# Rotary embedding in a fused decoder: exchanging the halves with a DVE shuffle instead of with products

## The reference, cut to what matters

```
def apply_rope(t, freqs):
    rot = freqs.shape[-1]                        # 32
    t1, tp = (t[..., :rot], t[..., rot:])
    d2 = rot // 2
    rh = jnp.concatenate([-t1[..., d2:], t1[..., :d2]], axis=-1)
    t1 = t1 * jnp.cos(freqs) + rh * jnp.sin(freqs)
    return jnp.concatenate([t1, tp], axis=-1)

q = (xq @ Wq).reshape(b, n, HEADS, DH).transpose(0, 2, 1, 3) * DH ** (-0.5)   # DH = 64: 0.125
k = (ctx @ Wk).reshape(b, j, HEADS, DH).transpose(0, 2, 1, 3)
v = (ctx @ Wv).reshape(b, j, HEADS, DH).transpose(0, 2, 1, 3)
q, k = apply_rope(q, pe_q), apply_rope(k, pe_k)
sim = jnp.where(mask, einsum('bhid,bhjd->bhij', q, k), -max)
out = einsum('bhij,bhjd->bhid', softmax(sim), v) -> reshape(b, n, 512) @ Wo + bo
```

## Time and profile before

| | |
|---|---|
| median of 3 runs | 4510.98 us (4506.9 to 4514.82) |
| the profiled execution | 4516.42 us, span of its trace 4514.8 us |
| PE busy | 89% of the span, 23856 matmuls |
| DVE / ACT / POOL busy | 59% / 44% / 19% |
| mean granted TensorE clock | 0.955 |

### The profile page before, as it was taken

How to read it: one execution, slowest core, us unless ns; L and a number is a source line. 1 busy time by engine, 2 the same in 40 slices (tenths; PEclk the granted TensorE clock), 3 DMA queues, 4 the chain that set the end, 5 groups by cost and what they waited for, 6 DMA issues and landing times. The chain is left out here.

```text
span 4514.8 us, 70500 instructions
## 1 busy us (share of the span) xinstructions
PE 4015.5 (89%) x23856; PEld 2483.2 (55%) x23856; DVE 2675.4 (59%) x7163; ACT 1998.7 (44%) x5804; POOL 860.4 (19%) x972
## 2 busy tenths in 40 slices
PE   6887799999999988889968877999999999888898
PEld 4644445655555555555646444565555555555555
DVE  3677566666666644654346775666666666456543
ACT  1732435555445434663227214454554444346632
POOL 2145221122221200000021452211122212000000
PEclk7999999999999998999969999999999999999999
DMA  2000000000000010010010000000000000100000
GB/s 68 24 16 1 16 7 16 22 16 22 16 22 1 25 54 19 7 57 8 1 57 5 16 1 16 7 16 22 16 22 16 22 2 24 54 20 34 30 8 10
DMA packets 15847, 91.84 MB, mean 20 GB/s; under 512 B 2176, under 2 KB 8064, under 8 KB 12032
## 3 DMA queue, kind: packets, MB, share of 16 engines
q1 hardware_dynamic: 15488, 87.27, 5.3%
HBM read 86.22 MB, written 1.05 MB: 19 GB/s over the span
## 5 line engine op out<-in xcount | busy, mean ns | idle before, releaser
L559 PE MATMUL ps_O<-wide,V 128*64 128x256 f32 (+4 forms) x5152 | 596.5, 394 | 1.9 <-ACT wide L583 1.8
L628 ACT ACTIVATE EX<-NB,neg 128x154 f32<-128x154 f32 (+3 forms) x640 | 350.2, 551 | 399.4 <-DVE neg L653 399.2
L601 POOL COPY RX<-recips 128x256 f32<-128x256 f32 (+2 forms) x356 | 156.8, 440 | 1822.9 <-DVE recips L668 1757.2
L679 DVE TENSOR_TENSOR QT<-ps_O,RS 128x512 f32<-128x512 f32 x212 | 146.6, 692 | 444.3 <-PE ps_O L559 444.3
L510 PE MATMUL ps_S<-KT,QT 64*128 64x154 f32 (+7 forms) x1936 | 368.0, 463 | 31.8 <-issue 21.5
L583 ACT ACTIVATE wide<-ps_P 128x512 f32<-128x512 f32 (+2 forms) x648 | 367.6, 569 | 60.9 <-PE ps_P L541 60.8
L394 POOL TENSOR_TENSOR small<-small 128x4 f32<-128x4 f32 x112 | 113.5, 1013 | 1467.8 <-DVE small L379 955.1
L541 PE MATMUL ps_P<-consts,EX 128*128 128x128 f32 (+1 forms) x2148 | 317.3, 281 | 80.0 <-ACT wide L583 41.5
L559 PEld LDWEIGHTS ps_O<-wide,V 128*64 128x64 f32 (+4 forms) x5152 | 266.9, 127 | 194.5 <-issue 110.7
L510 PE MATMUL ps_OUT<-KT,QT 64*128 64x154 f32 (+5 forms) x968 | 336.0, 441 | 0.4 <-ACT EX L628 0.4
L585 DVE COPY wide<-ps_P 128x512 f32<-128x512 f32 (+4 forms) x404 | 259.3, 643 | 117.9 <-PE ps_P L541 117.5
(11 more groups left out here) (345 smaller groups left out, 8154.1 us busy)
## 6 DMA issues: line engine op xcount, KB each, us to landing
weights<-in_w_dram SPq DMA_DIRECT2D x10, 1664.0 KB, 6.8
weights<-in_w_dram SPq DMA_DIRECT2D x2, 6148.0 KB, 17.5
weights<-in_w5next_dram SPq DMA_DIRECT2D x6, 1664.0 KB, 6.8
weights<-in_w_dram SPq DMA_DIRECT2D x2, 4200.0 KB, 13.0
weights<-in_reltab_dram SPq DMA_DIRECT2D x2, 4096.0 KB, 12.3
weights<-in_w_dram SPq DMA_DIRECT2D x8, 640.0 KB, 3.9
weights<-in_w_dram SPq DMA_DIRECT2D x5, 832.0 KB, 4.4
weights<-in_w_dram SPq DMA_DIRECT2D x2, 2050.0 KB, 8.0
```

The lines of the kernel that those rows point to most:

```text
L559: ins = pe.matmul(O1[self.slot * j:self.slot * (j + 1), q0 * P:(q0 + self.nq) * P], self.value(c * self.hpc + j, kc), self.probs(rd, j)[:, ...
L601: pool.tensor_copy(RX[:, q0 * P:(q0 + self.nq) * P].rearrange("p (n s) -> p n s", s=self.slot), of.unsqueeze(2).broadcast_to([P, self.nq * ...
L628: ins = act.activation(ex[:, a * N:(a + 1) * N], src, ACT.Exp, bias=neg[:, at:at + 1], scale=-1.0 if self.added else 1.0, accum_out=sums[: ...
L679: dve.tensor_tensor(self.out_chunk(c), O1[:, :], RS[:, c % 2, :], ALU.mult).then_inc(r.av_sb, 1)
```

## The change

The swapped products go. A chunk is now one row of the table, of the kind "rope": its product is read twice from the PSUM bank by DVE, first by a shuffle that exchanges lanes 0 to 15 with 16 to 31 in every group of 32 partitions and writes the part buffer, then by the multiplication with cos. POOL multiplies the part by sin (for queries by `sinq`, sin times 0.125, made once) and then, after a wait for its own result, adds. Groups of 32 channels that are not rotated are shuffled too; their sin is zero. Shuffle and cos row are evacuated in DVE's order; the shuffle of chunk j waits for POOL's rotation of chunk j - 4. In self steps the order of chunks is now k0, q0, k1, q1, ..., and scores of head pair c wait for 2c + 2 rotations; in cross steps it stays. All chunks still come before the first scores on PE and DVE. `fill2` goes: all value rows stand before the scores of round 1, the last one behind a wait for the next lane's `XT`, in self and cross steps. The weights are packed and loaded as before, the swapped ones too.

```
+        HALVES = [(m + 16) % 32 for m in range(32)]
+        def rope(dve, r, bank, dst, part, tables, wait):
+            if wait:
+                dve.wait_ge(*wait)
+            dve.stream_shuffle(part, bank, HALVES).then_inc(r.evac_dve, 1)
+            if tables[0] is None:
+                dve.tensor_tensor(dst, bank, tables[1], ALU.mult).then_inc(r.evac_dve, 1)
+            else:
+                dve.scalar_tensor_tensor(dst, bank, tables[0], tables[1], ALU.mult, ALU.mult).then_inc(r.evac_dve, 1)
...
-                self.order = [("k", c) for c in range(4)] + [("q", c) for c in range(4)]
+                self.order = [("k", c) for c in range(4)] + [("q", c) for c in range(4)] if cross else \
+                    [(m, c) for c in range(4) for m in "kq"]
...
-                                     queries=lambda c: (self.r.rotated, 4 + c + 1))
+                                     queries=lambda c: (self.r.rotated, 4 + c + 1 if cross else 2 * c + 2))
...
-                return [([(self.w("w" + m)[:, c * P:(c + 1) * P], x)], P, n, "D", kind, self.dest(m, c), cos),
-                        ([(self.w("swap" + m)[:, c * P:(c + 1) * P], x)], P, n, "D", kind, self.part[j % 4][:, 0:n],
-                         sin, (self.r.rotated, j - 3) if j >= 4 else None)]
+                return ([self.product(j)], P, n, "D", "rope", self.dest(m, c), (self.part(j), self.tables(j), self.before(j)))
+
+            def rotate(self, pool, j):
...
+                pool.wait_ge(r.evac_dve, 2 * j + 2)
+                pool.tensor_tensor(part, part, sin, ALU.mult).then_inc(r.sum_step, 1)
+                pool.wait_ge(r.sum_step, j + 1)
+                pool.tensor_tensor(d, d, part, ALU.add).then_inc(r.rotated, 1)
...
-                late = 0 if self.cross else 1
-                nv = len(self.values.rows) - late
+                last = len(self.mid.rows) - 1
                 def fill(pe):
-                    pe.wait_ge(r.evac_dve, self.tab.d)
+                    pe.wait_ge(r.evac_dve, self.front.d)
                     self.nxt.pe_head(pe)
-                    pe_table(pe, r, self.values, 0, nv)
-
-                def fill2(pe):
-                    if late:
-                        pe.wait_ge(self.nxt.r.xT, 1)
-                        pe_table(pe, r, self.values, nv)
+                    pe_table(pe, r, self.mid, 0, last)
+                    pe.wait_ge(self.nxt.r.xT, 1)
+                    pe_table(pe, r, self.mid, last)
...
-                    evacuate(dve, r, self.tab, "D", 0, 8)
+                    evacuate(dve, r, self.front, "D", 0, 4)
                     self.beside(dve, 0)
-                    evacuate(dve, r, self.tab, "D", 8, 12)
+                    evacuate(dve, r, self.front, "D", 4, 5)
                     self.beside(dve, 1)
-                    evacuate(dve, r, self.tab, "D", 12)
+                    evacuate(dve, r, self.front, "D", 5)
                 else:
                     self.beside(dve, 0)
-                    evacuate(dve, r, self.tab, "D", 0, 6)
+                    evacuate(dve, r, self.front, "D", 0, 3)
                     self.beside(dve, 1)
-                    evacuate(dve, r, self.tab, "D", 6, 12)
+                    evacuate(dve, r, self.front, "D", 3, 6)
                     self.beside(dve, 2)
-                    evacuate(dve, r, self.tab, "D", 12)
+                    evacuate(dve, r, self.front, "D", 6)
```

More of the change, by code:

```diff
@@ L142, in __init__ @@
                 d += 1
+                if r[4] == "rope":
+                    d += 1
             self.count.append((r[3], a if r[3] == "A" else d))
@@ L209, in build @@
         consts = sb("consts", [P, nconsts])
+        sinq = sb("sinq", [P, SEQ])
         lora_bias = sb("lora_bias", [P, 4])
@@ L344, in evacuate @@
                 if row[3] != who:
+                    continue
+                if row[4] == "rope":
+                    g = tab.j0 + j
+                    eng.wait_ge(r.proj, g + 1)
+                    rope(eng, r, RING[g % len(RING)][0:row[1], 0:row[2]], row[5], *row[6])
                     continue
@@ L1473, in __init__, with part, before, product @@
                 self.NK, self.src = NK, src
-                self.order = [("k", c) for c in range(4)] + [("q", c) for c in range(4)]
+                self.order = [("k", c) for c in range(4)] + [("q", c) for c in range(4)] if cross else \
+                    [(m, c) for c in range(4) for m in "kq"]
                 self.att = Attention(8, 64, NK, added=None if cross else (lambda h, qt: L.maskb[:, :]),
                                      keys=lambda c: KT[:, c, 0:NK],
-                                     queries=lambda c: (self.r.rotated, 4 + c + 1))
-                self.part = [wide[:, 2048 + SEQ * j:2048 + SEQ * (j + 1)] for j in range(4)]
+                                     queries=lambda c: (self.r.rotated, 4 + c + 1 if cross else 2 * c + 2))
+                ropes = [self.rotary(j) for j in range(8)]
                 values = [([(src[:, c * kc:(c + 1) * kc], w("wv"))], kc, SEQ, "A", "copy",
                            v_rows(kc, 8, 64, 64, c), None) for c in range(nch)]
-                self.tab = Table([row for j in range(8) for row in self.rotary(j)])
-                self.values = Table(values, self.tab)
+                self.front = Table(ropes)
+                self.mid = Table(values, self.front)
             def dest(self, m, c):
                 return QT[:, c, :] if m == "q" else KT[:, c, 0:self.NK]
+            def part(self, j):
+                at = 2048 + SEQ * (j % 4)
+                return wide[:, at:at + (SEQ if self.order[j][0] == "q" else self.NK)]
+            def before(self, j):
+                return (self.r.rotated, j - 3) if j >= 4 else None
+            def product(self, j):
+                m, c = self.order[j]
+                return self.w("w" + m)[:, c * P:(c + 1) * P], self.L.XT[:, :] if m == "q" else self.src[:, :]
+            def tables(self, j):
+                m = self.order[j][0]
+                n = SEQ if m == "q" else self.NK
+                return 0.125 if m == "q" else None, K("cos")[:, 0:n]
             def rotary(self, j):
@@ L1501, in pool @@
                 for j in range(8):
[L1502 to L1507, removed]
+                    self.rotate(pool, j)
+                self.att.pool(pool, self.r)
             def pe(self, pe):
@@ L1541, in fill @@
                     self.nxt.act_head(act)
-                    evacuate(act, r, self.values, "A")
+                    evacuate(act, r, self.mid, "A")
                 self.att.act(act, r, {1: [(r.rotated, 8)]}, fill)
@@ L2212, in _ @@
                 dve.tensor_scalar(scaled[:, 8:16], cols[:, a:a + 8], 0.125, None, ALU.mult).then_inc(s_boot2, 1)
-                dve.wait_ge(s_boot2, 3)
+                dve.tensor_scalar(sinq[:, :], K("sin"), 0.125, None, ALU.mult).then_inc(s_boot2, 1)
+                dve.wait_ge(s_boot2, 4)
         with nc.Fori(0, NBATCH // 2) as p:
```

17 lines of the change are left out of this document (9 added, 8 removed).

## The result

The changed kernel takes 4598.8 us (median of 4 runs, 4591.9 to 4611.3) against 4512.2 us before: ratio 1.0197, 95% interval 1.0171 to 1.0222. It is slower, by about 2%. The profiled execution took 4602.7 us, span 4601.0. The forecast was 4595, range 4515 to 4650.

A forecast was written before the change was run, and what follows sets the result against it. PE and DVE both near the bound in self steps, DVE in cross steps; 8 x (1.4 + 2.0 + 2.6 + 3.0) = +72 us, plus 12 for the clock, +84: 4600 profiled, 4595 median, range 4515 to 4650.

The forecast's parts named there:

- POOL's price and the shuffle's: Rotation of 512-column chunks: POOL's multiplication 1.27 us, the same as an addition; DVE's shuffle 0.65 us from start to start.
- DVE's five instructions behind POOL, the term that decides: DVE's normalising L407 and four L410 each wait about one POOL instruction; first score tile +1.0 us in self, lane 0.
- Rival A: DVE slips into the gap of POOL's pair, the five instructions stay at 2.3 us; 4476 to 4520 us, chance 0.14.
- The value wait: Last value row waits for ACT's XT copy before round 1 scores; transposes 7.1 us behind first tile (self), 6.4 (cross).
- (a) Self steps: Self-attention steps: +1.4 us per step in lane 0 and +2.0 in lane 1, eight steps each.
- (b) Cross steps: Cross-attention steps: +2.6 us per step in lane 1 and +3.0 in lane 0, eight steps each.
- 0.5 us in the 24 steps that don't have it yet: +12: PE's longer standing drops its granted clock to the 1.2 GHz level; 0.5 us per step, 12 us together.
- j4's new wait: Cross step, lane 1: j4's shuffle waits for POOL's j0 until 779.0; before, only its sin half waited, until 778.42.
- the port: DVE's small normalising instructions wait for POOL's; in the cross step L407 and the L410s run to 783.4.

The follow-up runs named there:

- Kernels 1: Changed kernel with the value rows back in their old places (`fill2` and its `late` rows restored); 1.0119 of the kernel before.
- kernel 7: Kernel before the change with only the new place of the value rows, all ahead of the scores of round 1; 1.0055 of the kernel before.
- kernels 2: Changed kernel with DVE's whole part for the neighbouring steps ahead of the chunks that POOL rotates; 1.0167 of the kernel before.
- kernel 10: Changed kernel with eight part buffers instead of four and nothing else; 1.0090 of the kernel before.
- Kernel 11: Changed kernel plus eight buffers, DVE's neighbouring parts first, short cross keys by products, values first only in self steps, last cross query product repeated four times; 0.9938.
- kernel 12: Changed kernel with PE repeating the last query product of cross steps four more times into the same bank; 1.0218 of the kernel before.

## Why the prediction was right, and where it was not

**POOL's price and the shuffle's: right.** 1.27 to 1.28 us for the multiplication, 0.62 us from start to start for the shuffle where 0.65 was taken. The mask's load is 0.014 us. The estimate from the Trainium skill ("VectorE: DVE Perf Modes", section "The perf-mode tier table"), 0.11 us more than a multiplication, is not borne out: the trace shows 0.02 more. The page's figures are for 2048 columns, and the prediction took their whole difference over to 512; by an estimate from the same row, a quarter of it, 0.03, would have fitted.

**DVE's five instructions behind POOL, the term that decides: right in place and size.** The first score tile was forecast 849.85 - 833.17 = 16.68 us behind the first product and came at 860.12 - 843.54 = 16.58. In lane 1 the tile was forecast 1.7 us later than before and came 1.66 later, and in 14 of the 16 cross steps 1.69 later (1.65 forecast). Rival A (DVE slips into POOL's gap) fell: the group took 5.04 us with the gap there. Its price was a little too good, too: it took 1.2 us for a chunk where the forecast took 1.25, and left out that the last shuffle would wait for POOL's j3. By the prediction's own times that ends at 846.1, which puts the first tile at 847.35, 1.5 us earlier than before and not 1.9.

**The value wait: right in the cross step, and in the self step only up to the transposes.** From tile to transposes 7.17 us in the self step (7.1 said), 6.38 in the cross step (6.4 said). From POOL's power to the transposes, the cross steps grew by 2.63 and 3.03 us (2.6 and 3.0 said). Kernels 1 and 7 confirm it as a separate cost, of 35 and 25 us; the prediction's terms for it come to 24. But it had 0.3 to 0.4 us of them in each self step. That is there at the transposes and is given back behind them: kernel 7 has self steps 0.3 us shorter, and all of the cost in the cross steps.

**What the sum mis-sized, with errors that cancelled.** (a) Self steps: 27 us and a share of the clock were put in, 21 came. At the transposes the usual step of lane 0 is 1.26 late (1.4 said), but 0.7 is given back right behind them: the value rows are evacuated sooner, and the third transposes no longer wait 0.66 us for ACT. In lane 1 the transposes are 2.0 late, as said, and the step is 1.1 longer. I had called the stretch behind the transposes almost gapless. The first self step of each turn, in which two shuffles waited for part buffers (2.56 and 1.24 us), cost about 4 instead of 1.4; this I hadn't worked out. (b) Cross steps: 45 us and 4 of clock were put in, 60.5 came. The steps where the clock lay as in the one worked out have 2.5 to 2.9; others up to 6.3. The term "0.5 us in the 24 steps that don't have it yet: +12" was too small for them: about 15 us in the 16 cross steps alone, if all that comes behind the first tile beyond the forecast is put down to the clock, as the slow stretches there suggest. That the sum of 84 us met the 86 measured is in part luck.

**One sentence of the mechanism was incomplete.** I named j4's new wait (2.28 us measured) and then the port as the terms of the cross step, and took the part buffers for no bound in the self step. In the usual self step that is so as the kernel stands, but kernels 2 and 10 show them as the next bound: take away the port alone and 14 us come back, the buffers alone 48, both 81 (1.0197 to 1.0017). In usual self steps it takes both edits, in cross steps either does. POOL's lateness is one cause with two doors.

**Left open.** The clock's share of the 86 us was not isolated. Kernel 11 shows about 21 us for it where PE stood mainly in one place, kernel 12 that the same repair does nothing where there are three. The new order of chunks in self steps (k0, q0, k1, ...) was not tested by itself, and the kernel before was not given the edits that helped the changed one.

## What to carry to other kernels

Work taken from TensorE and put on GpSimd is not free because GpSimd was at 19%: what counted here is which DVE instructions with all operands in SBUF stand beside it, and how many buffers lie between the two engines. Remove one such wait and look which other was as late; here two doors had to be opened together, with a few idle buffers and a changed order, to turn +2.0% into +0.2%, and the value rows put back to get to -0.2%. And where TensorE stands still in several places of a stage, filling one of them can move the slow clock from where it hurts nobody to where it does, as in the cross step of kernel 12.

## What the runs showed of the hardware

- A shuffle of 128x512 float32 out of PSUM: 0.73 us, 0.62 from start to start; of 154 columns 0.33. Loading its mask: 14 ns.
- DVE's scalar_tensor_tensor of 128x128, alone 0.34 us, took 1096 to 1416 ns each beside a POOL that never paused, and 0.52 us each beside POOL's short instructions of 154 columns (2.08 for four in kernel 10). Shuffles and cos rows, which read PSUM, were not held up: at most 0.74 and 0.69 us in the whole trace.
- Repeating a product into the same bank costs PE 0.86 us and, where it filled the one long stand before the scores, gave about 21 us back through the clock.
